# VectorE's order inside a turn of a four-layer graph network: the row operation ahead of the accumulation

## What is computed

```python
# block 0, three times: msg = relu(x[src] + edge_attr_16 @ emb); mean over dst; two 64x64 products
# block 1, twice:       msg = edge_weight * x[src];               sum over dst;  two 64x64 products
# block 2:              sum over dst of x[dst] * edge_attr_64
# block 3, three times: attention with 8 heads:
e = leaky_relu(alpha_s[src] + alpha_d[dst])
e_exp = exp(e - segment_max(e, dst)[dst])
msg = (e_exp / segment_sum(e_exp, dst)[dst]) * h[src]
out = segment_sum(msg, dst)
```

## Time and profile before

| what | value |
|---|---|
| median of 3 runs | 17362.4 us (17359.42 to 17365.91) |
| profiled execution, first to last instruction | 22236.9 us |
| busy: PE / PE weight load / DVE / ACT / POOL | 48% / 43% / 31% / 17% / 56% of the span |
| granted PE clock, mean | 0.511 of full speed |
| passes in the profiled span | sage0 100 to 2712, sage1 2848 to 5320, sage2 5410 to 7882, gin0 8018 to 10381, gin1 10450 to 12800, gat0 12973 to 15940, gat1 16032 to 19023, gat2 19115 to 22110 |

### The profile page before, as it was taken

The page is one execution under the profiler, slowest core; times in us unless marked ns, Lnnn a source line. Parts: engine busy times, 40 slices in busy tenths (PEclk is TensorE's granted clock), DMA queues, the critical chain, the costliest instruction groups (busy, mean ns, idle before and its releaser), DMA issues. The chain is left out here.

```text
span 22236.9 us, 220022 instructions
## 1 busy us (share of the span) xinstructions
PE 10574.4 (48%) x59536; PEld 9523.6 (43%) x59537; DVE 6788.2 (31%) x17499; ACT 3759.7 (17%) x5833; POOL 12396.4 (56%) x12932
## 2 busy tenths in 40 slices
PE   5777744444444421112111155555655555655555
PEld 5666634443444411111111145555455555455554
DVE  1111111111111111111111155555555555555555
ACT  0000000000000000000000033333333333333333
POOL 4555456665666646665666635555455555455553
PEclk5555555555555555555555555555555555555555
DMA  2222111111111111111111112222122222122221
GB/s 47 46 46 47 40 26 27 27 27 25 27 27 27 27 20 23 23 23 23 23 23 23 23 45 57 56 57 56 48 56 56 55 56 56 49 56 56 55 56 41
DMA packets 1022298, 881.00 MB, mean 40 GB/s; under 512 B 725873, under 2 KB 727665, under 8 KB 1022235
## 3 DMA queue, kind: packets, MB, share of 16 engines
q0 software_dynamic: 413696, 444.31, 11.0%
q1 hardware_dynamic: 608539, 435.96, 6.7%
HBM read 865.07 MB, written 14.17 MB: 40 GB/s over the span
## 5 line engine op out<-in xcount | busy, mean ns | idle before, releaser
L626 POOL DMA_INDIRECT rows<-node_table,idx x6464 | 6188.8, 957 | 3914.5 <-issue 1961.1
L1262 POOL DMA_INDIRECT rows<-gat_table,idx x4848 | 4680.8, 966 | 4606.8 <-DVE msg L1458 2707.4
L655 PE MATMUL bank<-sel,msg 128*64 128x48 f32 x10720 | 1292.5, 308 | 4484.4 <-DVE msg L691 1961.8
L655 PEld LDWEIGHTS bank<-sel,msg 128*64 128x64 f32 x10720 | 1194.0, 224 | 4582.8 <-DVE accT L668 1747.8
L1293 PE MATMUL bank<-avm,bufB 48*128 48x16 f32 x9696 | 2098.4, 363 | 630.3 <-ACT avm L1339 453.9
L1293 PEld LDWEIGHTS bank<-avm,bufB 48*128 48x128 f32 x9696 | 2033.6, 316 | 694.7 <-ACT avm L1339 469.5
L1417 DVE CUSTOM_DVE_ANT_0 far<-scores,far 128x1024 f32<-128x1024 f32 x1818 | 2129.3, 1221 | 487.4 <-remote 420.7
L626 POOL DMA_INDIRECT rows<-in_x,idx x1616 | 1526.6, 945 | 1162.9 <-issue 529.6
L1348 ACT ACTIVATE far<-bufA,subcol 128x1024 f32<-128x1024 int32 x1818 | 2063.4, 1147 | 508.1 <-issue 244.8
L655 PE MATMUL scores<-sel,msg 128*64 128x48 f32 x5440 | 655.9, 308 | 2272.9 <-DVE msg L691 968.1
L668 DVE TENSOR_TENSOR accT<-accT,bank 64x48 f32 x670 | 131.9, 197 | 5104.8 <-remote 3997.3
(11 more groups left out here) (150 smaller groups left out, 11092.9 us busy)
## 6 DMA issues: line engine op xcount, KB each, us to landing
bufA<-in_dst_rows SPq DMA_DIRECT2D x606, 512.0 KB
rows<-node_table,idx POOLq DMA_INDIRECT x6464
rows<-gat_table,idx POOLq DMA_INDIRECT x4848
bufA<-in_attr SPq DMA_DIRECT2D x202, 256.0 KB
bufB<-in_attr SPq DMA_DIRECT2D x606, 64.0 KB
idx<-in_src SPq DMA_DIRECT2D x1616, 4.0 KB
rows<-in_x,idx POOLq DMA_INDIRECT x1616
node_table<-tbuf SPq DMA_DIRECT2D x52, 128.0 KB
```

What stands on the lines that cost most here:

```text
L626: nc.gpsimd.indirect_dma_start(rows[s][:, j, 0:D], None, table, bass.IndirectOffsetOnAxis(idx[s][:, j:j + 1], 0)).then_inc(s_rows[s].handl ...
L655: last = nc.tensor.matmul(bank[3 + s][0:D, 0:WIN], msg[s][:, j, 0:D], sel[s][:, j, :], start=j == 0, stop=j == G - 1)
L1262: nc.gpsimd.indirect_dma_start(rows[s][:, j, :], None, gat_table, bass.IndirectOffsetOnAxis(idx[s][:, j:j + 1], 0)).then_inc(s_rows[s].han ...
```

## The change

Two blocks of DVE's program move; no instruction is added or removed, and no wait condition changes. In `sum_pass` the call of `add_sums(g - 1)` moves behind the row operation of group g. In `gat_pass` the message product of group g-1 moves ahead of the transposed selection of group g.

```diff
                         nc.vector.tensor_tensor(sel[s][:], ..., ALU.is_equal).then_inc(q["sel_ready"].handle, 1)
-                        if not (isinstance(g, int) and g == 0):
-                            add_sums(g - 1, (s - 1) % R)
                         ve.wait_ge(s_rows[s].handle, s_rows[s].at((it + 1) * 16 * G))
...
                                                     bc(wgt[:, ds(g, 1), :]...), ALU.mult
                                                     ).then_inc(q["msg_ready"].handle, 1)
+                        if not (isinstance(g, int) and g == 0):
+                            add_sums(g - 1, (s - 1) % R)
...
+                        if has(g, 1):
+                            ve.wait_ge(q["p_ready"].handle, q["p_ready"].at(g))
+                            nc.vector.tensor_tensor(msg[before]..., rows[before]..., ALU.mult
+                                                    ).then_inc(q["msg_ready"].handle, 1)
                         if real:
                             ve.wait_ge(s_bA[s].handle, s_bA[s].at(it * 16 + 16))
...
                             nc.vector.tensor_scalar(bufB[s][0:WIN, :], ..., ALU.subtract, ALU.is_equal).then_inc(q["selT_ready"].handle, 1)
-                        if has(g, 1):
-                            ve.wait_ge(q["p_ready"].handle, q["p_ready"].at(g))
-                            nc.vector.tensor_tensor(msg[before]..., rows[before]..., ALU.mult
-                                                    ).then_inc(q["msg_ready"].handle, 1)
```

More of the change, by code:

```diff
@@ L1449, in body @@
                             nc.vector.tensor_tensor(z[:], ed[:, :, H:2 * H], z[:], ALU.subtract).then_inc(q["z_done"].handle, 1)
+                        if has(g, 1):
+                            ve.wait_ge(q["p_ready"].handle, q["p_ready"].at(g))
+                            nc.vector.tensor_tensor(msg[before][:, :, 0:D].rearrange("p j (h c) -> p j h c", c=C),
+                                                    rows[before][:, :, 0:D].rearrange("p j (h c) -> p j h c", c=C),
+                                                    bc(msg[before][:, :, D:ROW], [P, G, H, C], 3), ALU.mult
+                                                    ).then_inc(q["msg_ready"].handle, 1)
                         if real:
@@ L1455, in body @@
                                                     ALU.subtract, ALU.is_equal).then_inc(q["selT_ready"].handle, 1)
-                        if has(g, 1):
-                            ve.wait_ge(q["p_ready"].handle, q["p_ready"].at(g))
-                            nc.vector.tensor_tensor(msg[before][:, :, 0:D].rearrange("p j (h c) -> p j h c", c=C),
-                                                    rows[before][:, :, 0:D].rearrange("p j (h c) -> p j h c", c=C),
-                                                    bc(msg[before][:, :, D:ROW], [P, G, H, C], 3), ALU.mult
-                                                    ).then_inc(q["msg_ready"].handle, 1)
                         if has(g, 2):
```

## The result

| | median us | runs |
|---|---|---|
| kernel before | 17363.21 | 4 runs, 17359.42 to 17365.91 |
| changed kernel | 17666.32 | 4 runs, 17658.43 to 17671.43 |

The changed kernel is slower: ratio 1.0175 [1.0162, 1.0187], some 303 us. The forecast was 17,710 us in a range of 17,400 to 17,900, with 0.82 on slower. The profiled execution of the changed kernel has a span of 17655.8 us; the run that was profiled took 17658.43.

The account below looks back on a forecast made before the run. The prediction took POOL's bare issue of indirect transfers to bound the timed runs. It summed 17,362 + 125 (sage0) + 100 (other sum passes) + 120 (attention) + 2 (ends) = 17,709, forecast 17,710 us, range 17,400 to 17,900.

Parts of the forecast that it names:

- What bounds the kernel: Whole kernel: POOL issues transfers without a pause in the timed runs, explaining all but 120 us of 17,362.
- the 4,875 us: Profiled execution before the change: its extra length over the timed median, taken as waits that only the profiled execution has.
- Sage0's ring: sage0: PE's aux waits for DVE's add, now behind the row add; turn 10.63 us against POOL's 10.0, +125 us.
- if the register work hides: sage0, cheapest case: accT add 0.6 us behind the row add instead of 1.0, so +45 us.
- `sel` in the other sum passes: sage1, sage2, gin0, gin1: the later sel starts just before a POOL transfer and delays it; +100 us, bounds 0 and 200.
- Attention: gat passes: bufB, moved behind the product, runs across a POOL transfer's start and delays it; +120 us, bounds -120 and +200.
- The trade that was taken as possible: Attention: the 120 us left of the median probably sit here and may be exchanged for the new delay of +200.
- DVE's own turn grows to 9.35 us: Attention: bufB no longer fills the product's wait for ACT, so DVE's turn goes from 8.62 to 9.35 us, under POOL's 10.0.
- Only the loop of sage0 counts: Rival, 17%: sel starts just late enough and attention trades like for like; about 17,490 us.
- Nothing shows: Rival, 11%: PE runs sage0 at 2.4 GHz in the timed runs and the overlaps are free; 17,365 us.
- Faster: Rival, 7%: bufB ahead of the first transfer is the 120 us, the change removes it, sage0 costs 45; 17,287 us.
- DVE becomes the bound in attention: Rival, 5%: DVE's attention turn is really above 10.3 us, adding 442 us; about 18,100 us.

Follow-up runs that it names:

- load_ahead_2: The changed kernel with the register load of the window's start ahead of the wait for the rows in all five sum passes: 17558.17 us, 1.0112 of before.
- best: The kernel before, with attention's order made message product, two adds of add_sums, then bufB: 17366.06 us, 1.0002 of before.
- sel_first: The kernel best with attention's sel one small operation earlier, ahead of subpick: 17350.09 us, 0.9993 of the kernel before.
- pe_padded: The kernel before with 24 empty instructions on PE ahead of its loop in each of the eight passes: 17363.43 us, 1.0 of before.

## Why the prediction was right, and where it wasn't

**What bounds the kernel.** Right: in the trace of the first kind POOL's turn takes 9.99 to 10.01 us in the sum passes and 10.15 to 10.17 in attention, and its excess over the bare issue is 120 us, as worked out. Wrong was the sentence on the 4,875 us, "I take them for the profiled execution's own". On chips of the second kind the timed runs have them too (22162.5 to 22275.96). What sage0's sum took from that trace, durations and distances inside undisturbed turns, held on both kinds.

**Sage0's ring.** Right in every link. Row add 3.71 us behind `ea` (forecast 3.71), `accT` add 0.92 behind that (about 1.0), `auxT` add 0.13 (0.12), `aux` 0.35 (0.35), `sums` 3.55 (3.57), `ea` 1.88 (1.88): 10.54 against 10.63. The term mis-sized is the register work, 0.92 for 1.0. Over the whole pass `ea` follows `ea` after 10.555 us on average, before 10.010: 201 x 0.545 = 110 us, and +109.4 was measured for the pass, against +125. `load_ahead_2` puts the bound "if the register work hides" at +43.7 us for sage0 (2201.5 - 2157.8), where the prediction had +45.

**`sel` in the other sum passes.** The mechanism is right, with a transfer of 1.28 us where `sel` starts 0.10 ahead of it, and free in the turns that end the body. The size was half: 50.6 us for 100. In these four passes some 150 transfers were held by `sel`, by 0.35 us on average, out of 808 turns; the forecast amounts to a third of them. In most of the turns inside the body `sel` came just too late: it starts between 0.06 us before the transfer and 0.1 after it, and from 0.03 before on (some 290 of these turns) the transfer loses nothing. That is the margin of 0.05 us of which the prediction had warned, and the term lay within its bounds of 0 and 200.

**Attention.** The sum was near (+136.2 for +122), and two of its steps were wrong. The first is the rule that an operation which starts after the transfer's start costs nothing. It was read from a product, and it holds for the products, and for `sel` to 0.04 us, but not for `bufB`. The prediction placed `bufB` 0.19 us behind the transfer and called that "free, or at most a small part"; at such a distance it costs 0.17, and together these cases make 71 us. With them `bufB` holds 99 us before the change, 0.16 us a turn of the 0.18 that the prediction found left over. The second is `sel`, which it called free after the change ("itself 0.3 late, starts at 10.3"); `sel` costs 57 us in attention. `bufB` itself was sized well: 182 / 606 = 0.30 us a turn, forecast 0.33. The trade that was taken as possible (-120 to +200) happened: the 71 us of a `bufB` about to start went away, and so did the 28 of before, for the 182. That the errors nearly cancel is luck. That the place of `bufB` is the cause is shown by `best`, which takes the price away by no more than two small adds ahead of it, 0.4 us. That DVE's own turn grows to 9.35 us can't be seen where POOL sets the pace: the product waits 1.77 us for ACT before and 1.85 after (medians), not 0.5 and 1.3.

The rule of the Trainium skill, SBUF — State Buffer, section "SBUF: two separate sides", of an exclusive lock between VectorE and GpSimd fits the direction: the row add, with one input in PSUM, held none of the 71 transfers that started under it, while `sel` and `bufB` did. That whoever starts first has the lock doesn't fit the transfers that are late though `bufB` starts behind them. Its warning is that GpSimd can't write descriptors while a VectorE operation runs in a two-port mode. If `bufB` is such an operation, which no view shows, the transfers of 0.94 us under a `bufB` begun within 0.15 us before them don't fit it.

**The rivals.** *Only the loop of sage0 counts* (17,490) is excluded by +186.8 us in the seven other passes. *Nothing shows* needed the higher clock; the windows show 0.50, the 1.2 GHz level, in sage0 on both kinds of chip, with PE busy 1,895 of 2,267 us. *Faster* held that `bufB` is the 120 us and that the change takes them out. The first is nearly so (99 us), though mostly with `bufB` behind the transfer's start and not before it; the second isn't, since `bufB` moved onto another transfer and holds 182 there. *DVE becomes the bound in attention* fails since POOL's idle time there is unchanged to some 2 us.

**Still open.** Why a `bufB` about to start holds a transfer, and why one that has just begun doesn't. What strings out PE's instructions on chips of the second kind, and why a pass that wasn't edited differs by some per cent between kernels there; whether the kind belongs to the chip itself isn't shown. That the place of code in memory has a part in it was suspected and not tested.

## What to carry to other kernels

A block moved behind a wait takes its register loads and its semaphores with it: follow each value that it releases round the ring, and compare the ring with the bound's turn. When POOL's issue is the bound, an operation on DVE costs nothing by the turn's length, but by where it starts and ends against a transfer's start; 0.4 us of shift were worth 133 us of POOL's time. Look at every distance before you call one free: a rule read from one operation (a product behind the transfer costs nothing) failed for another (`bufB`). And an expected saving of that kind must be worked out with the phase that it moves: `sel_first` saved 13 us of 60.

## What the runs showed of the hardware

- A transfer of 0.94 us that starts while `bufB` is under way goes on about 0.12 us before that ends: with 0.3, 0.4, 0.5 and 0.6 us of `bufB` left it is late by 0.19, 0.27, 0.38 and 0.47 on average (586 transfers of the changed kernel). `sel` (0.56 us) and the products (0.69) do the same. An operation that has only just begun costs nothing: `bufB` begun 0.15 us or less before the transfer (350 transfers of `best`, `bufB` up to 0.02 behind included, late by 0.01 at most), `sel` begun less than 0.03 before.
- A `bufB` that starts 0.05 to 0.38 us behind a transfer's start makes it late by that distance less 0.016 us: 358 of 358 transfers in `pe_padded`, 184 of 184 in `best`, 439 of 439 in `sel_first`, whatever was under way. More than 0.43 us off it costs 0.04 at most (88 transfers of `pe_padded`). The products cost nothing when they start behind it, `sel` 0.04 at most. Why isn't known.
- The row add, with one input in PSUM, held none of 71 transfers in the changed kernel.
- Register work between two operations costs 0.92 - 0.60 = 0.32 us when it isn't hidden under a wait.
- The same program takes 17,360 us on one chip and 22,200 on three others, at about the same granted clock (mean 0.503 to 0.513 in all runs).
